# A two-block sequence model on one core: the shared expert moved to the last phase, attended rows one tick ahead, powers between scatters, loads and inversions moved into attention

## The reference, cut to what matters

```
out = softmax(Q K^T / 4, causal) V            # heads of 16, then @ W_o
x   = x + out @ W_o
xf  = layernorm(x)
shared = silu(xf @ Sg) * (xf @ Su) @ Sd       # Sg, Su: 256 x 256, Sd: 256 x 256
top_p, top_i = top_k(softmax(xf @ Wr), 2)     # 16 experts
routed = sum over the 2 chosen of top_p * (silu(xf @ Wg[e]) * (xf @ Wu[e]) @ Wd[e])
result = x + routed + shared
```

## Time and profile before

| what | us |
|---|---|
| median of three runs | 1931.21 |
| the profiled execution, whole | 1926.69 |
| its span in the profile | 1924.9 |
| attention | 923.6 to 1501.6 |
| back | 1501.6 to 1695.8 |
| second run of experts (m1) | 1695.8 to 1838.9 |
| finish | 1838.9 to 1924.9 |
| PE, DVE, ACT, POOL busy over the span | 1601.7, 1022.4, 705.2, 565.6 |

### The profile page before, as it was taken

The page is one execution under the profiler, slowest core; times in us unless marked ns, Lnnn a source line. Parts: engine busy times, 40 slices in busy tenths (PEclk is TensorE's granted clock), DMA queues, the critical chain, the costliest instruction groups (busy, mean ns, idle before and its releaser), DMA issues. The chain is left out here.

```text
span 1924.9 us, 28980 instructions
## 1 busy us (share of the span) xinstructions
PE 1601.7 (83%) x9337; PEld 1074.9 (56%) x9337; DVE 1022.4 (53%) x2851; ACT 705.2 (37%) x1457; POOL 565.6 (29%) x993
## 2 busy tenths in 40 slices
PE   1999999955999996885599999999999299869910
PEld 0577777643666664543355555555554178758810
DVE  1344544451222222786677777777773268855533
ACT  0444444411222221222056666666667011134400
POOL 2222443341000002784312322222323135500056
PEclk9899999977999998897799999999999689979965
DMA  8000111112121213685845655655650655445444
GB/s 303 27 22 30 51 53 45 45 66 82 63 67 63 66 58 117 186 284 193 141 57 80 102 78 81 105 84 85 98 81 26 176 186 158 146 145 157 149 133 148
DMA packets 151056, 204.02 MB, mean 106 GB/s; under 512 B 20608, under 2 KB 119424, under 8 KB 150656
## 3 DMA queue, kind: packets, MB, share of 16 engines
q1 hardware_dynamic: 104304, 131.12, 30.5%
q10 hardware_dynamic: 34320, 37.50, 5.7%
q0 software_dynamic: 12288, 33.57, 5.4%
HBM read 116.91 MB, written 84.93 MB: 105 GB/s over the span
## 5 line engine op out<-in xcount | busy, mean ns | idle before, releaser
L1690 DVE CUSTOM_DVE_ANT_0 t_seen<-t_ps_s,t_later 128x1024 bf16<-128x1024 f32 (+7 forms) x512 | 375.2, 757 | 148.8 <-PE t_ps_s L1736 145.9
L1707 ACT ACTIVATE t_probs<-t_ps_st 128x512 f32<-128x512 f32 x576 | 330.1, 597 | 189.9 <-PE t_ps_st L1751 185.4
L1751 PE MATMUL t_ps_st<-t_qs,t_ks 128*128 128x512 f32 (+3 forms) x768 | 262.3, 390 | 0.8 <-ACT t_probs L1707 0.5
L1667 POOL TENSOR_SCALAR_AFFINE_SELECT t_probs<-t_probs 128x128 f32<-128x128 f32 x512 | 139.5, 302 | 358.9 <-ACT t_probs L1707 357.7
L1736 PE MATMUL t_ps_s<-t_ks,t_qs 96*128 96x512 f32 (+3 forms) x768 | 239.8, 366 | 4.5 <-DVE t_row_max L1690 4.2
L1751 PEld LDWEIGHTS t_ps_st<-t_qs,t_ks 128*128 128x128 f32 x768 | 132.9, 190 | 136.6 <-ACT t_probs L1707 102.3
L1767 PE MATMUL t_ps_o<-t_probs,t_vs 128*17 128x256 f32 (+1 forms) x2560 | 185.0, 363 | 2.3 <-POOL t_probs L1667 1.8
L1349 POOL DMA_INDIRECT d_ye<-outputs_dram,r_pos_all x64 | 64.3, 1004 | 325.9 <-POOLq L1112 308.1
L1736 PEld LDWEIGHTS t_ps_s<-t_ks,t_qs 96*128 96x128 f32 x768 | 134.4, 191 | 34.7 <-DVE t_row_max L1690 23.6
L849 PE MATMUL ps_h<-w_in,xnt 128*128 128x512 f32 x256 | 125.4, 614 | 22.9 <-ACT xnt L683 22.9
L1144 PE MATMUL m_ps_h<-w_sb,m_xt 128*128 x284 | 135.4, 599 | 0.0
(11 more groups left out here) (312 smaller groups left out, 2672.1 us busy)
## 6 DMA issues: line engine op xcount, KB each, us to landing
m_x_t<-gathered_dram SPq DMA_DIRECT2D x150, 128.0 KB, 2.0
outputs_dram<-m_y ACTq DMA_DIRECT2D x150, 128.0 KB, 1.7
t_qs<-qkt_dram SPq DMA_DIRECT2D x128, 128.0 KB, 5.5
t_ks<-qkt_dram SPq DMA_DIRECT2D x128, 128.0 KB, 5.8
qkt_dram<-d_hi SPq DMA_DIRECT2D x32, 256.0 KB, 4.1
qkt_dram<-d_lo SPq DMA_DIRECT2D x32, 256.0 KB, 4.1
headst_dram<-t_att SPq DMA_DIRECT2D x32, 256.0 KB, 7.5
x_t<-in_x_dram SPq DMA_DIRECT2D x8, 512.0 KB, 4.7
```

Source lines behind the costliest of these rows:

```text
L1667: nc.gpsimd.affine_select(out=diag, in_=diag, compare_op=ALU.is_ge, fill=0.0, base=0, pattern=[[1, P]], channel_multiplier=-1).then_inc(ma ...
L1690: nc.vector.tensor_tensor_reduce(out=seen[:, i % 2, 0:width], in0=ps_s[i % 2][:, 0:width], in1=later[:, NC * P - width:], scale=1.0, scala ...
L1707: nc.scalar.activation(probs[:, p % 2, i // NST, base:base + STC], ps_st[i % 2][:], ACT.Exp, scale=HD ** -0.5).then_inc(exp_ready, 1)
L1751: last = nc.tensor.matmul(ps_st[i % 2][:, col:col + width], ks[:, at, kc * P:(kc + 1) * P], qs[:, at, q0:q0 + width], start=True, stop=True)
```

## The change

1. **attention**: at the start of tick 4 ScalarE issues the two 2 MB loads of `wgu_sb`. After the last pair's units, the sums of batches 0 to 2 are loaded, inverted in one VectorE instruction and stored from there. The mask tile `later` becomes bf16.
2. **back, start**: loads of groups 0, 1 and 2 are issued at once; only batch 3 is inverted here, in tick 2. W_o and the router weights are issued by ScalarE. The 2 MB of `wd_sb` and 0.75 MB of shared-expert weights are issued by ScalarE before its third group.
3. **back, tick**: the shared expert is gone. W_o is applied one group ahead with two PSUM buffers; `scale` runs two groups ahead on the same ring of three loads. Normalising moves to ScalarE (Identity with scale and bias), and VectorE makes the bias (`centre`). `choose` stands behind `measure`. GpSimd scatters a group three ticks behind, two DMAs, then the power, then two DMAs. The transposed rows of all groups are kept on chip (`xnt_all`).
4. **end of back and of front**: the list is made by a chain of 11 instructions on 128 partitions and two small transposing matmuls; correcting the places and the softmax weights move into `run_experts`, as `settle`, on VectorE between tiles 5 and 17. One list entry fewer is made.
5. **finish**: the shared expert for a group of two tiles runs beside the gathers, and one VectorE addition per group and one store of 256 KB per group close it.

```diff
 # attention, ScalarE
             for tick in range(pairs + 3):
+                if tick == 4:
+                    fetch(act)
 # attention, VectorE, behind the last pair
+            dve.wait_ge(sums_loaded, 16 * (BATCH - 1))
+            nc.vector.reciprocal(sums, sums).then_inc(inv_ready, 1)
 # back, GpSimd
-            for tick in range(NG + 2):
+            for tick in range(NG + 3):
+                if live(tick - 3):
+                    scatter(tick - 3, 0)
                 if live(tick):
                     rsqrt(tick)
-                if live(tick - 2):
-                    scatter(tick - 2)
+                if live(tick - 3):
+                    scatter(tick - 3, 1)
 # back, VectorE
             for tick in range(NG + 2):
-                if live(tick - 2):
-                    choose(tick - 2)
                 if live(tick):
                     add_res(tick)
                     measure(tick)
                 if live(tick - 2):
-                    add_shared(tick - 2)
-                if live(tick + 1):
-                    scale(tick + 1)
+                    choose(tick - 2)
                 if live(tick):
-                    normalise(tick)
+                    centre(tick)
+                if live(tick + 2):
+                    scale(tick + 2)
+                if tick == 2:
+                    invert()
                 if live(tick - 2):
                     place(tick - 2)
-                if live(tick - 1):
-                    gate(tick - 1)
 # back, ScalarE
-            act.wait_ge(w_loaded, 64)
-            fetch(act)
             for g in range(NG):
+                if g == 2:
+                    fetch(act)          # wd_sb, then the three shared weights
+                normalise(g)
                 copy_x(g)
-                sigmoid(g)
 # back, TensorE
+            attend(0)
             for tick in range(NG + 2):
-                if live(tick):
-                    attend(tick)
+                if live(tick + 1):
+                    attend(tick + 1)
                 if live(tick - 1):
                     turn_x(tick - 1)
                 if live(tick - 2):
-                    go_down(tick - 2)
                     rank(tick - 2)
                 if live(tick - 1):
-                    go_up(tick - 1)
                     weigh(tick - 1)
 # run_experts, VectorE
             for i in range(n_list + 3):
+                late(dve, i)            # settle(dve, nc, kept, i)
 # finish, VectorE (new)
+            def gate(g):
+                dve.wait_ge(sig_ready, g + 1)
+                nc.vector.tensor_tensor(act_g[:, g % 2], ps_g[g % 2][:], sig[:, g % 2], ALU.mult)
+                dve.wait_ge(u_done, g + 1)
+                nc.vector.tensor_tensor(ht[:, g % 2], ps_u[g % 2][:], act_g[:, g % 2], ALU.mult)
+            def combine(g):
+                dve.wait_ge(gathered[g % R], ...)
+                # four scalar_tensor_tensor of 128x256, then
+                nc.vector.tensor_tensor(y[:, g % 2], total[:, g * G:(g + 1) * G, :], ps_y[g % 2][:], ALU.add)
+            for tick in range(NG + 1):
+                if live(tick):
+                    gate(tick)
+                if live(tick - 1):
+                    combine(tick - 1)
 # finish, TensorE (new)
+            for tick in range(NG + 1):
+                if live(tick):
+                    wait(pe, gated, tick - 1)
+                    go_up(tick)
+                if live(tick - 1):
+                    go_down(tick - 1)
```

More of the change, by code:

```diff
@@ L241, in front @@
     end = sb("end", [P, E])
[L242 to L247, removed]
-    pad_row = sb("pad_row", [1, E], U32)
[L251 to L255, removed]
+    place_no = sb("place_no", [P, 1])
+    room = sb("room", [P, E])
+    passed = sb("passed", [P, 2, E])
+    sums_of = sb("sums_of", [P, 2])
+    entry = sb("entry", [P, 2])
+    pad_row = sb("pad_row", [1, E], U32)
     ps_h = [pb(f"ps_h{h}", [P, DI]) for h in range(2)]
@@ L333, in _ @@
             sp.wait_ge(list_ready, 1)
-            for e in range(E):
-                at = sp.value_load(pad_row[0:1, e:e + 1], min_val=e * CAP, max_val=e * CAP + TOK)
-                sp.dma_start(gathered[bass.ds(at, P), :], zeros[:]).then_inc(padded, 16)
+            for e0 in range(0, E, 4):
+                rows = nc.values_load_multi_w_load_instructions(
+                    pad_row[0:1, e0:e0 + 4], engines=[sp.engine], min_val=0, max_val=(E - 1) * CAP + TOK,
+                    skip_runtime_bounds_check_because="a row is a region's start and a count of at most all tokens")[1]
+                for at in rows:
+                    sp.dma_start(gathered[bass.ds(at, P), :], zeros[:]).then_inc(padded, 16)
             for s in range(2):
@@ L653, in _ @@
[L653 to L661, removed]
@@ L1070, in _, with run_experts @@
                     new_state(q)
+            pe.wait_ge(entry_ready, 2)
+            for i in range(2):
+                last = nc.tensor.matmul(ps_list[0:1, i, :], entry[:, i:i + 1], ident[:], start=True, stop=True)
+            last.then_inc(list_done, 1)
 RING = 6
-def run_experts(nc, sb, pb, sem, c, name, E, gathered, outputs, kept, up, down, weights):
+def run_experts(nc, sb, pb, sem, c, name, E, gathered, outputs, kept, up, down, weights, late):
     ident = c["ident"]
@@ L1868, in back @@
[L1868 to L1882 removed]
+    place_no = sb("k_place_no", [P, 1])
@@ new lines, in back @@
+    room = sb("k_room", [P, E])
+    passed = sb("k_passed", [P, 2, E])
+    sums_of = sb("k_sums_of", [P, 2])
+    entry = sb("k_entry", [P, 2])
+    pad_row = sb("k_pad_row", [1, E], U32)
+    ps_wo = [pb(f"k_ps_wo{s}", [P, G, DM]) for s in range(2)]
+    ps_xnt = [pb(f"k_ps_xnt{s}", [P, KD, G * P]) for s in range(2)]
+    ps_l = pb("k_ps_l", [P, 2 * DM])
+    ps_logits = ps_l[:, 0:G * E].rearrange("p (j e) -> p j e", e=E)
+    ps_r = pb("k_ps_r", [P, 2 * DM])
+    ps_rank = ps_r[:, 0:(G + 1) * E]
@@ L1883, in back @@
         "list_ready", "padded"))
-    sums_loaded = [sem(f"n_sums_loaded{b}") for b in range(BATCH)]
-    inv_stored = [sem(f"n_inv_stored{b}") for b in range(BATCH)]
     x_loaded = [sem(f"n_x_loaded{s}") for s in range(R)]
-    scattered = c["moved"]["r1_scattered"]
+    scattered = [sem(f"n_scattered{s}") for s in range(X)]
     def live(g):
```

543 lines of the change are left out of this document (286 added, 257 removed).

## The result

The changed kernel takes **1880.9 us** (median of four runs, 1876.5 to 1882.0) against 1929.9 beside it: ratio 0.9741, 95% interval 0.9719 to 0.9763. The forecast was 1883. Its profiled execution took 1880.1 us with a span of 1878.4. On which chip it ran is not on record.

| stage | before | after | difference | forecast |
|---|---|---|---|---|
| front | 449.9 | 448.9 | -1.0 | 0 |
| first run of experts | 300.1 | 302.3 | +2.2 | 0 |
| project_qkv, clearing | 173.6 | 173.8 | +0.2 | 0 |
| attention | 577.9 | 579.0 | +1.1 | +5.5 |
| back | 194.2 | 139.8 | -54.4 | -59 |

What follows compares the result with a forecast made beforehand. TensorE bounds back, and GpSimd would after the change. Back -59, attention +5.5, second experts +1.8, finish +3.7 give -48: profiled 1926.7 to 1878.7, and 1883 us as the profile lay 4.5 below the median; 8-in-10 range 1866 to 1902.

Steps and rivals of the forecast that it cites:

- Back, -54.4 for -59: Back: earlier loads and a GpSimd-bound tick make it 59 us shorter, bounds 44 to 67 us less.
- 3 us for slow loads: Back: 3 us added because residual loads are slowed by 2.75 MB of weights.
- between 5.87 and 6.9: Back, tick: 6.2 us taken, between GpSimd's 5.87 us of work and 6.9 us with TensorE at half clock.
- TensorE's half clock: Rival, back: TensorE at half clock binds with 6.9 us ticks, 1894 us in all; chance 0.15.
- The loads become the bound: Rival, back: loads landing late make ticks 7.25 us, 15 us more, 1898 in all; chance 0.10.
- The 4 MB didn't collide: Rival, attention: the 4 MB collide with the pairs' loads and TensorE waits, 14 us more, 1897; chance 0.08.
- Finish never fell to the half clock: Rival, finish: it runs at TensorE's half clock, 78 us more, 1961 in all; chance 0.03.
- Only moved: Rival, finish: the shared expert only moves, slower gathers and lockstep waits add 16 us, 1899; chance 0.04.
- Attention, +1.1 for +5.5: Attention: 5.09 us of weight issuing on ScalarE makes TensorE stand and its clock fall, +5.5 us, bounds +3 and +12.
- Second run of experts, +2.0 for +1.8: Second run of experts: added VectorE instructions between tiles make the gate late, +1.8 us, bounds 0 and +4.
- Finish, +3.5 for +3.7: Finish: GpSimd sets the pace; +2.2 us at the end and 1.5 for slower gathers, bounds +1 and +9.
- The last addition that I counted: Finish, end: one further addition behind the last group's four instructions, 0.7 us of the +2.2.

Runs made afterwards that it cites:

- finish_bare: Changed kernel whose finish leaves out the shared expert (no matmuls, sigmoid or gate; output lacks it): 1877.1 us, ratio 0.9738.

## Why the prediction was right

**What bounds.** Right: back was TensorE's, becomes GpSimd's, and the experiment that gives TensorE its work back brings GpSimd's waits back.

**Back, -54.4 for -59.** The pieces: the last scatter 131.3 us behind the first load, forecast 127.3; then 8.5 us to the barrier, forecast 7.5. Of the 4 us missing 2.4 are the start (first scatter at 30.7 instead of 28.3). My "3 us for slow loads" was right in size: VectorE waited 4.05 us for loads, and GpSimd stood 3.61. What I had put at next to nothing is ScalarE's issue, which I had called mostly hidden because normalising runs ahead of the ranks; it does, by less than 7 us, and GpSimd stood 3.50. In the other two profiles of this kernel the same issue took 7.57 and 8.95 us for 4.36; GpSimd stood 6.40 and 7.27 there, and at most 1.57 at a time behind it, so there the issue is most of it.

**Back, tick: right size, wrong reason.** I took 6.2 us "between 5.87 and 6.9" for TensorE's clock. The tick is 6.25, and the clock has no part in it: GpSimd has no gap over 0.31 us in these ticks, so its own instructions fill them, and the tick from 1612.9 to 1618.7 took 5.76 us at a granted clock of 0.50, those at 0.81 took 6.25. The 0.5 us are VectorE's scaling, both of whose operands lie in SBUF, at the start of the scatter. I had read 1.04 behind a power from front, where no such instruction runs. The Trainium skill (SBUF — State Buffer, "SBUF: two separate sides") states that such a VectorE instruction and a GpSimd one that reads SBUF take turns on one pair of ports; the traces agree (1.52 for 1.04, 1.24 for 0.72; in 206 of 209 cases GpSimd's instruction is longer by the rest of VectorE's less 0.13 us). It should have been weighed, with the scatters of 1.81 and 1.45 us in the trace of before beside it.

**Rivals.** TensorE's half clock does not bind: see the tick above. The loads become the bound in the first ticks only (one wait of 4.05 us, 1547.6 to 1551.6), not in the steady ones. The 4 MB didn't collide: TensorE has no wait there beyond the 2.57 us. Finish never fell to the half clock for long (0.98 over the stage). "Only moved" fell with finish_bare.

**Attention, +1.1 for +5.5.** The mis-sized term. I charged the whole 5.09 us of the earlier trace rows as a block; here the two issues took 0.44 and 3.29, with an exponential between them, TensorE lost one wait of 2.57 us, and its clock stayed full. In the twelve profiles that load in attention this wait is 1.09 to 2.57 us, and the stage takes 577.8 to 583.3 us by the barriers, against 578.0 and 577.0 in the two that don't. The waits thus show a cost of 1 to 3 us; what makes up the rest of that spread stays open.

**Second run of experts, +2.0 for +1.8.** Not shown: from first load to first load this stage took 142.2 to 144.5 us in the twelve runs and the profile after, and 143.1 before. A match within the spread. The first run's +2.2 likewise: the last addition falls at 747.8 us in both traces, and from first load to first load the stage took 299.7 before and 299.8 to 301.2 after.

**Finish, +3.5 for +3.7.** Right size. The slower gathers are there (2.1 us here, 64 x (0.982 - 0.949), where I took 1.5), from one gather in most groups that starts under the additions and not from a busy VectorE as such. From the last gather's start to the end takes 7.8 us instead of 6.5, +1.4 where I took 2.2. The last addition that I counted (0.7) isn't seen: with and without it the stage differs by 0.2 us.

So the total was right by the large term, back, and by errors that cancel: +4.6 there, -4.4 in attention. That it hit within 3 us is luck, and so is where it was measured: the same kernel took 1906.1 us on chip 6, outside my range of 1866 to 1902, and the prediction has no term for the pauses.

## What to carry to other kernels

When a long engine is relieved, list what each engine starts behind each of the others' instructions: the next bound's durations come from rows with other neighbours than it will have. A DMA issued by a computing engine behind others can hold that engine for many times what it takes alone, and not for the same time in each run, so issue weights where nothing waits behind them. Compare a variant only with a control on the same chip, also where the kernel before shows no difference between chips.

## What the runs showed of the hardware

- The same program takes 1878 us on one chip and 1906 on another. On three of four chips (one group of runs on each) ScalarE, VectorE and TensorE pause up to 11 us before instructions whose inputs are there, in front, project_qkv, back and finish, where GpSimd's indirect transfers run beside them; finish takes 107 to 112 us instead of 89. The cause isn't shown. The kernel before is within 0.2% on all of them. The change's gain is thus 2.6% on one chip and 1.3% on the other.
- A scatter, gather or power of GpSimd that starts under a VectorE instruction with two operands in SBUF takes longer by what is left of that instruction less 0.13 us (206 of 209 cases): 0.5 us right behind the start of a scaling of 0.69 us, up to 0.27 for a gather under the additions of finish. With an operand in PSUM nothing is added (381 cases).
- A weight load behind others takes longer to issue: 2 MB took 0.37 to 0.44 us with none ahead of it, 1.81 to 5.97 behind 2 MB, and 12.48 and 14.91 behind 4 MB. The queue alone doesn't set it: 256 KB behind 2 MB took 4.23 to 8.95 us in seven profiles and 1.92 to 2.17 in five, and 6.27 behind 6 MB.
